# Second layer of a graph network: edges gathered in sorted tiles of 128 rows and summed on TensorE

## The reference, cut to what matters

```python
def _L2_gnn_ref(x, edge_index, edge_weight, eps):
    row, col = (edge_index[0], edge_index[1])     # src, dst
    w = jnp.where(row != col, edge_weight, jnp.zeros_like(edge_weight))
    msgs = w[:, None] * x[col]
    agg = jax.ops.segment_sum(msgs, row, num_segments=x.shape[0])
    return (1.0 + eps[0]) * x + agg
...
h = jnp.maximum(_layernorm(x, axis=-1), 0.0)
x = x + _L2_gnn_ref(h, edge_index, edge_weight, L2_gnn_eps)
```

## Time and profile before

| | |
|---|---|
| median of 3 runs | 7946.03 us |
| the profiled execution, its span | 7948.8 us |
| POOL busy | 4309.1 us, 54% |
| PE matmul busy | 4702.6 us, 59% |
| DVE busy | 4461.4 us, 56% |
| ACT busy | 1261.5 us, 16% |
| DMA | 644.26 MB, mean 81 GB/s |

### The profile page before, as it was taken

One profiled execution on the slowest core, in us unless ns is written; L12 is line 12 of the kernel. 1 busy time (PEld: TensorE's weight loads), 2 busy tenths in 40 slices (PEclk: granted clock), 3 DMA queues, 4 the chain that ended last, 5 costly groups with the idle time before them and its releaser, 6 DMA issues. The chain is left out here.

```text
span 7948.8 us, 124234 instructions
## 1 busy us (share of the span) xinstructions
PE 4702.6 (59%) x28437; PEld 3515.5 (44%) x28438; DVE 4461.4 (56%) x14642; ACT 1261.5 (16%) x4005; POOL 4309.1 (54%) x3463
## 2 busy tenths in 40 slices
PE   6589888888888888860038665532222222209696
PEld 5344455555555555540038555432222222208585
DVE  7878666666666666659532667754444444431313
ACT  0023333333333333330000000000000000000101
POOL 0046667666666667660220678777777777740000
PEclk5578867777776777665569555555555555559898
DMA  0001221211221221136527333332222222219191
GB/s 20 1 11 35 59 38 39 59 38 39 57 40 38 39 58 39 37 74 236 162 112 301 70 81 79 83 73 61 61 61 61 57 62 62 57 22 364 43 372 41
DMA packets 612266, 644.26 MB, mean 81 GB/s; under 512 B 396280, under 2 KB 549008, under 8 KB 576519
## 3 DMA queue, kind: packets, MB, share of 16 engines
q1 hardware_dynamic: 471760, 500.71, 20.1%
q0 software_dynamic: 134272, 89.36, 7.5%
q10 hardware_dynamic: 6118, 53.08, 2.0%
HBM read 425.43 MB, written 213.96 MB: 80 GB/s over the span
## 5 line engine op out<-in xcount | busy, mean ns | idle before, releaser
L374 POOL DMA_INDIRECT sorted_rows<-rows,place_i x1600 | 2093.9, 1309 | 1180.0 <-issue 608.7
L1294 POOL DMA_INDIRECT gathered_rows<-feature_table,gather_index x1600 | 2008.1, 1255 | 518.1 <-issue 473.6
L1372 PE MATMUL block_total<-attr_half,block_hot 125*128 125x65 f32 x4192 | 955.9, 421 | 1554.3 <-DMA attr_half<-in_edge_attr_dram 1544.5
L1372 PEld LDWEIGHTS block_total<-attr_half,block_hot 125*128 125x128 f32 x4192 | 912.7, 331 | 1598.4 <-issue 1391.9
L538 PE MATMUL part<-high,low 125*128 x3612 | 1405.3, 528 | 109.6 <-DVE high L414 103.3
L414 DVE TENSOR_TENSOR high<-iota_g,window_keys 125x1568 f16 x903 | 875.2, 969 | 7.4
L1330 DVE TENSOR_SCALAR block_hot<-iota_f,block_keys 125x128 f32<-125x128 f32 x2096 | 604.3, 352 | 425.2 <-PE block_total L1372 264.8
L526 PE MATMUL count_rows<-counts,lo_rows_f 128*125 128x49 f32 x3200 | 761.4, 328 | 0.0
L538 PEld LDWEIGHTS part<-high,low 125*128 x3612 | 436.8, 121 | 683.6 <-issue 613.6
L395 DVE CUSTOM_DVE_ANT_0 picked<-count_rows,oh_hi 125x49 bf16<-125x49 f32 x1600 | 314.0, 235 | 740.8 <-PE count_rows L527 647.7
L526 PEld LDWEIGHTS count_rows<-counts,lo_rows_f 128*125 128x125 f32 x3200 | 673.5, 260 | 92.4 <-issue 87.3
(11 more groups left out here) (343 smaller groups left out, 5496.3 us busy)
## 6 DMA issues: line engine op xcount, KB each, us to landing
piece_round<-slabs SPq DMA_DIRECT2D x140, 1120.0 KB, 7.2
slabs<-slab SPq DMA_DIRECT2D x20, 3920.0 KB, 19.7
piece_conv<-slabs SPq DMA_DIRECT2D x70, 1120.0 KB, 5.2
attr_half<-in_edge_attr_dram SPq DMA_DIRECT2D x262, 250.0 KB
scanned<-scan_out ACTq DMA_DIRECT2D x10, 4480.0 KB
scanned<-message_sums SPq DMA_DIRECT2D x50, 896.0 KB
sorted_rows<-rows,place_i POOLq DMA_INDIRECT x1600
gathered_rows<-feature_table,gather_index POOLq DMA_INDIRECT x1600
```

The lines of the kernel that those rows point to most:

```text
L374: pool.indirect_dma_start(sorted_rows[:, :], bass.IndirectOffsetOnAxis(ap=place_i[:, h, u:u + 1], axis=0), rows[:, h, u, :], None).then_in ...
L1294: pool.indirect_dma_start(got[b][:, j, :], None, table[:, :], bass.IndirectOffsetOnAxis(ap=index[b][:, j:j + 1], axis=0)).then_inc(gathere ...
L1372: nc.tensor.matmul(total[b][:, :], hot[:, j, :], attr[j // HALF][:, j % HALF, :], start=False, stop=True, skip_group_check=True).then_inc( ...
```

## The change

`scan_messages` becomes `sum_messages`. The sorted edges are seen as 1563 tiles of 128, padded to 1568 (98 groups of GT = 16). POOL gathers a group into one of RING = 8 places of `got`: it reads the group's entry of `turn_table` into a register (the source block in which group n - 8 ends), waits until PE has used that group, copies 16 target numbers per partition, issues 16 indirect DMAs of 128 rows, then waits for the landing of the group before and adds 1 to `landed`. DVE makes, for each tile, a 128 x 128 matrix that holds the edge's weight in the column of its source node (one tensor_scalar, is_equal then mult, against a row of numbers 0 to 6271), in four buffers. PE multiplies it with the gathered rows into PSUM. A visit has VT = 4 tiles; source block i goes over the visits first to last from `src_table`, so a visit that lies across a border is done for both blocks. ACT copies the block's sum to `agg`. In each turn i of 49, every engine does source block i, then target block i of `attr_sum` as before (one PSUM bank in place of five), each with a register load of its own. Scans, weighting, `scanned` stores, carries and the second `gather_runs` go; x gets `agg` added.

For this layout the keys are needed with the edge number across partitions: `scan_sorted` keeps `src_sorted` as well, and `edge_statistics_layer` stores the three arrays to HBM, loads them as rows of 128, turns them on PE (39 transposes, 4 matmuls for the last edge of each tile) and copies them to `src_rows`, `dst_rows`, `w_rows`; this stands ahead of the wait for `gather_runs` on DVE. Only added lines are shown, cut to the core: SP's part and one of the turning loops, the tables, then of `sum_messages` POOL's part, DVE's and PE's source visits; the target visits that follow in each turn are those printed above, and what is replaced is `scan_messages`.

```diff
+GT = 16
+SG = 2 * HI
+ST = SG * GT
+SBLK = -(-ST // P)
+STAIL = ST - (SBLK - 1) * P
+DUMMY = HI * P - 1
+RING = 8
+VT = 4
...
+                same = same_src[:, :]
+                nc.vector.tensor_copy(g["src_sorted"][:, k * J:(k + 1) * J], src_c)
...
+            for c, name in enumerate(("src_sorted", "dst_sorted", "w_sorted")):
+                two_parts(sp, sorted_keys[c, 0:E].rearrange("(p j) -> p j", p=EP), g[name][:, :], keys_stored)
+            sp.wait_ge(pads_ready, 3)
+            sp.dma_start(sorted_keys[:, E:ST * P].unsqueeze(0), pads[:, :, :]).then_inc(keys_stored, 16)
+            sp.wait_ge(keys_stored, 7 * 16)
+            for c in range(3):
+                rows = sorted_keys[c, :].rearrange("(t e) -> t e", e=P)
+                whole = (SBLK - 1) * P
+                sp.dma_start(key_rows[:, c, 0:SBLK - 1, :], rows[0:whole, :].rearrange("(b t) e -> t b e", t=P)
+                             ).then_inc(keys_loaded, 16)
+                sp.dma_start(key_rows[0:STAIL, c, SBLK - 1, :], rows[whole:ST, :]).then_inc(keys_loaded, 16)
...
+            for c, name in enumerate(("src_rows", "dst_rows", "w_rows")):
+                for q in range(KQ):
+                    k, first = KQ * c + q, 4 * q * P
+                    cols = min(4 * P, ST - first)
+                    dve.wait_ge(keys_ready, k + 1)
+                    nc.vector.tensor_copy(g[name][:, first:first + cols],
+                                          keys_turned[k % 2][:, :, :].rearrange("p a b -> p (a b)")[:, 0:cols]
+                                          ).then_inc(keys_copied, 1)
...
+            dve.wait_ge(keys_copied, 4 * KQ)
+            step(nc.vector.tensor_single_scalar(g["turn_table"][:, RING:RING + SG], lasts[:, GT - 1:ST:GT], 7,
+                                                ALU.arith_shift_right))
+            step(nc.vector.tensor_copy(g["src_table"][:, 0:HI], g["start"][0:1, 0:HI]))
+            step(nc.vector.memset(g["src_table"][:, HI:HI + 1], E))
+            step(nc.vector.tensor_single_scalar(g["src_table"][:, :], g["src_table"][:, :], 9, ALU.arith_shift_right))
...
+        hot_src = [s.sb(f"hot_src{j}", [P, P], F32) for j in range(VT)]
+        iota_n = s.sb("iota_n", [P, HI * P], F32)
...
+        LANDED = 16 * GT
+        FREE = GT * RING + VT
...
+        def visits(engine, i):
+            _, v = nc.values_load_multi_w_load_instructions(g["src_table"][0:1, bass.ds(i, 2)], engines=[engine],
+                                                            min_val=0, max_val=E // (VT * P),
+                                                            skip_runtime_bounds_check_because=RANGES)
+            return [x & 1023 for x in v]
 
         @block.gpsimd
         def _(pool):
+            pool.iota(iota_n[:, :], pattern=[[1, HI * P]], base=0, channel_multiplier=0,
+                      allow_small_or_imprecise_dtypes=True).then_inc(iota_ready, 1)
+
+            def group(n, r, k, first=False):
+                _, v = nc.values_load_multi_w_load_instructions(g["turn_table"][0:1, bass.ds(n, 1)],
+                                                                engines=[mybir.EngineType.Pool], min_val=0,
+                                                                max_val=HI - 1, skip_runtime_bounds_check_because=RANGES)
+                pool.wait_ge(hot_used, GT * n + VT * (v[0] & 63) + GT + VT)
+                pool.sem_inc(pool_turns, 1)
+                pool.tensor_copy(index[k][:, :], g["dst_rows"][:, bass.ds(n * GT, GT)]).then_inc(index_ready, 1)
+                pool.wait_ge(index_ready, n + 1)
+                pool.sem_inc(pool_turns, 1)
+                for j in range(GT):
+                    pool.indirect_dma_start(got[:, (k * GT + j) * D:(k * GT + j + 1) * D], None, table[:, :],
+                                            bass.IndirectOffsetOnAxis(ap=index[k][:, j:j + 1], axis=0)
+                                            ).then_inc(gathered[k], 16)
+                if k:
+                    pool.wait_ge(gathered[k - 1], LANDED * (r + 1))
+                elif not first:
+                    pool.wait_ge(gathered[RING - 1], LANDED * r)
+                pool.sem_inc(landed, 1)
+
+            for k in range(RING):
+                group(k, 0, k, True)
+            with pool.Fori(1, SG // RING) as r:
+                for k in range(RING):
+                    group(r * RING + k, r, k)
+            for k in range(SG % RING):
+                group(SG - SG % RING + k, SG // RING, k)
+            pool.wait_ge(gathered[SG % RING - 1], LANDED * (SG // RING + 1))
+            pool.sem_inc(landed, 1)
 
         @block.scalar
...
+            with dve.Fori(0, HI) as i:
+                first, last = visits(DVE, i)
+                with dve.Fori(first, last + 1) as q:
+                    t = nc.s_assert_within(q * VT, 0, ST - VT, skip_runtime_bounds_check_because=RANGES)
+                    v = q + i
+                    for j in range(VT):
+                        dve.wait_ge(hot_used, v * VT + FREE - VT + j + 1)
+                        nc.vector.tensor_scalar(hot_src[j][:, :], iota_n[:, bass.ds(i * P, P)],
+                                                g["src_rows"][:, bass.ds(t + j, 1)], g["w_rows"][:, bass.ds(t + j, 1)],
+                                                ALU.is_equal, ALU.mult).then_inc(hot_ready, 1)
+                before, offset = load_ranges(nc, g["blk_table"], DVE, i, 1, MOST)
...
+            pe.sem_inc(copied, 1)
+            pe.sem_inc(agg_copied, 1)
+            pe.sem_inc(hot_used, FREE)
+            with pe.Fori(0, HI) as i:
+                first, last = visits(PE, i)
+                pe.wait_ge(agg_copied, i + 1)
+                nc.tensor.matmul(ps_agg[:, :], g["zerob"][:, 0:P], g["zerob"][:, 0:D], start=True, stop=True)
+                with pe.Fori(first, last + 1) as q:
+                    v = q + i
+                    pe.wait_ge(landed, (q >> 2) + 2)
+                    for j in range(VT):
+                        pe.wait_ge(hot_ready, v * VT + j + 1)
+                        nc.tensor.matmul(ps_agg[:, :], hot_src[j][:, :],
+                                         got[:, bass.ds(((q & (RING * GT // VT - 1)) * VT + j) * D, D)], start=False, stop=True,
+                                         skip_group_check=True).then_inc(hot_used, 1)
+                before, _ = load_ranges(nc, g["blk_table"], PE, i, 1, MOST)
...
+                step(nc.vector.tensor_tensor(x[:, :, :], x[:, :, :], agg[:, :].rearrange("p (b f) -> p b f", f=D), ALU.add))
...
+    sorted_keys = nc.dram_tensor("sorted_keys", [3, ST * P], F32)
+        with ExitStack() as to_turn:
+            kept_sorted(nc, to_turn, g)
+            scan_sorted(nc, g, sorted_rows, scanned, carries)
+            locate_runs(nc, g)
+            edge_statistics_layer(nc, g, scanned, carries, sorted_keys, x, u, w1, b1, w2, b2)
+        weighted_layer(nc, g, table, eps, edge_attr_64)

```

240 lines of the change are left out of this document (97 added, 143 removed).

## The result

The changed kernel takes 8896.47 us (median of four runs, 8891.88 to 8916.54) against 7943.73 us for the kernel before (7925.15 to 7952.92): 1.1208 times as long, 95% interval 1.1188 to 1.1228. I had predicted 7660 us. The 12% lie in one stage, and they belong to one kind of chip: on two of the six chips of the experiments the kernel does not lose them. Unchanged it ran on one of these two, and took 0.931 of the kernel before there.

The account below looks back on a forecast made before the run. POOL's gathers bound the old loop; PE's in-order chain (2400 us) would bound the new one. 7948.8 - 287 + 3 = 7665 us profiled, 7660 as median; range 7470 to 7930.

Parts of the forecast that it names:

- Gather: POOL's 128-row gathers in the new loop: 0.944 + 0.304 = 1.248 us each, with row count as the likeliest cause.
- The group of 21.9 us: POOL's 16 gathers of 1.248 us plus 1.96 us for index copy and register load; 98 groups are 2148 us.
- The rival of 1.51 us: POOL's gather stays at 1.51 us because the loop is the cause; group 26.2 us, time 7880 to 7960; 12%.
- PE's chain: PE's in-order work in the weighted layer: 1080 target + 1067 source + 181 blocks = 2328 us, 2400 with the start.
- Source side: PE's source tiles in the weighted layer: 439 visits of 2.43 us, 1067 us.
- Blocks: PE's two register loads of 1.6 us and a clearing matmul each per block: 3.7 us, 181 in all.
- Target side: PE's 130 target visits in the weighted layer: 49 at 7.33 us and 81 at 8.9, 1080 us.
- the rival in which POOL is the bound: PE's clock rises, source visit 1.7 us, target visit 7.2, so POOL is the bound: 7410 to 7550; 16%.
- the source visit: Four source tiles in the loop over `q`: 4 x 0.458 + 0.6 = 2.43 us; ends 1.7 and 3.5.
- the source visit is slow: Loop over `q`: DVE address work, semaphores and PE's branch don't overlap; 3.5 us a visit, time 8125; 12%, milder case 6%.
- DVE locks POOL out: Each new DVE one-hot holds a POOL gather for 0.22 us, 386 us on POOL, time about 7910; 2%.
- The small things: Source copy in scan_sorted +3 us; turning the sorted keys covered by DVE's 110 us wait, 0 us, uncovered 75.

Follow-up runs that it names:

- the first profile: The changed kernel, unedited, profiled in the first comparison with the kernel before, on a chip that stalls: 8896.47 us against 7943.73, 1.1208.
- the control: The changed kernel without any edit, run in the third group on a chip that does not stall: 7265.95 us against 7797.43 for the kernel before, 0.9314.
- e3: The changed kernel with two POOL memsets of 128x64 behind each gather, against the kernel before: 8571.15 us, 1.0798.
- the fourth group's control: The changed kernel without any edit, run in the fourth group on a stalling chip: 8880.63 us against 7949.82 for the kernel before, 1.1175.

## Why the prediction was wrong, step by step

**Gather: right.** 0.944 + 0.304 = 1.248 us taken; 0.946 us of work in the first profile and 0.955 in the control, 1.25 us apart in both. The group of 21.9 us is 20.9 in the control (median): beyond its gathers it takes 0.8 us, not 1.96, and only POOL's early waits bring the mean to 21.7. The cause that I named, the row count, was only half right: 112, 120 and 128 rows take 937, 986 and 946 ns, 124 and 125 rows 1298 and 1215. It goes with the number of shares (16, 15, 16; 4, 5), not with the number of rows. The rival of 1.51 us is out for this layout.

**PE's chain: 453 us too long.** 1875 us measured against 2328. Source side 803 against 1067: I had put 0.6 us between visits, read from the target side's changes, and it isn't there; the wait and the branch pass while matmuls are still running, and a visit is 1.83 to 1.86 us. Blocks 40 against 181: the register loads hide in the same way, 0.8 us instead of 3.7. Target side 1032 against 1080. So even where nothing stalls I had the bound wrong: POOL's 2129 us set the end, not PE's 2400. The kernel became 531 us shorter (7797.43 - 7265.95), not 284, and 0.9314 x 7943.73, an estimate, is 7399 us, under the low end of my range. That is 11 us under the rival in which POOL is the bound, but not by its cause: the granted clock stayed at 0.50, the 1.2 GHz level, in the whole loop.

**The step that failed: the source visit, with its hand-over between DVE and PE put at nothing.** I took 2.43 us a visit, with both semaphore passes of a tile hidden under PE's 0.458, and 3.5 at the upper end. I had costed the passes at what they cost beside 125-row gathers, and no row of the kernel before showed them beside a stream of 128-row ones. Where the chip stalls, a source tile beside the gathers took 3.70 us, four of them 14.8, and the loop took 3647 us in place of the 2400 that I had for it. With one gather in 16, on a chip that stalls, the same visit took 1.85; with all gathers, on a chip that doesn't, a tile took 0.427. The rival "the source visit is slow" had the right place (the loop over `q`), the right sign and 3.5 us a visit at most. Its condition, that four buffers don't hide the round trip, was what the trace showed, with a round trip far over any that the rows ahead of the prediction held. I should have asked of "the gather becomes 0.27 us shorter" not only what POOL gains but what else then happens more often.

**DVE locks POOL out: no.** In the control the longest of 1568 gathers is 1072 ns beside 1756 one-hots, the median 947. The rule of the Trainium skill, page "SBUF — State Buffer", section "SBUF: two separate sides", which spoke against the change, cost nothing that this trace shows with one-hots of 128 columns. In the first profile it was DVE that waited beside POOL's transfers, not the other way round.

**The small things held.** In the first profile the turning of the keys ended at 3988.3 and the wait for the run gathers lasted until 4033.6 with 45.3 us to spare: 0 us, though the stall had eaten much of its cover. The tail is gone: in the control the last target product ends at 6429.2 and the layer's add starts at 6429.9.

## What to carry to other kernels

When a transfer is re-cut so that it gets shorter and follows its forerunner sooner, its own time is the smaller part: look on the timeline at how long the semaphores of the other engines take beside it, and if a price comes from a few such transfers in a quiet stretch, let the range hold both a chip that delays the semaphores and one that doesn't. When a run is meant to change a pace, measure the pace that it got: the memsets of `e3` moved it by 0.11 us only, and so it doesn't part the two theories. Carry the unchanged kernel through every group of runs as a control; without it, "120 rows cure it" would stand here as a finding. And before adding an overhead per visit, see whether the engine is idle at such a change at all: PE's own chain hid 400 us of them.

## What the runs showed of the hardware that I had not expected

- Chips differ, for one program, by more than the change is worth. The first comparison and the groups on four chips showed the kernel before at 7936 to 7954 us and a stall; two chips showed 7790 and 7797 and none (the copies of turned keys show it on all of them). The 150 us that the kernel before differs by lie ahead of the weighted layer (`iota_n` starts at 4413.4 in the first profile and at 4263.5 in the control). Each chip was seen once, so a property of the chip and one of that hour can't be told apart.
- On the chips that stall, increments arrive up to 13.6 us late, in the stretch read above, beside gathers of 15 or 16 shares 1.25 to 1.29 us apart (dense tile 3.54 and 3.70 us); a tile takes 2.14 us where they are 1.36 apart, and 0.46 beside gathers of 5 shares 1.51 apart. The lateness isn't there at once; it grows over the first 20 us of gathering.
- The trace records fewer increments there: between 5000 and 5500 us, of the gathers' semaphores, 399 for the 192 gathers of the fourth group's control, which posted 3072 four-byte packets; in the third group's control 6133 for 6127. With 125 rows on a stalling chip it is 2152 for 5097. Where increments are late they are also seldom seen. The data packets themselves are hardly slower: 126 ns in the median in the fourth group's control, 116 in the third's.
- Open: what delays the increments, whether it goes by the pace of the gathers or by the number of their shares, and why fewer waits and increments buy so little. 128-row gathers 1.5 us or more apart, and 10 or 8 shares, weren't tried on a stalling chip. Nor can the recording be ruled out as a part of it: each execution here, those behind the medians too, has a recorded span and clock, and the chips that stall are those whose traces lack increments. Whether the stall exists in an execution that nothing records, no run here shows.
